# Delta stage written out cycle by cycle, with two places for solved rows, values projected last, and the residual added in the MLP stage

## The reference, cut to what matters

```python
h = rms(x)                                   # x: rows after attention
q, k, v = (silu(silu(causal_conv(h @ W.T))) for each of q, k, v)   # 4 taps
q, k = l2norm per head of 16; beta = sigmoid(h @ Wbeta.T)          # 32 heads
for t in range(32):                          # per sequence and head
    S = S - beta_t * (S k_t - v_t) k_t^T
    o_t = S q_t
x = x + rms(o) @ Wout.T
x = x + (silu(rms(x) @ Wgate.T) * (rms(x) @ Wup.T)) @ Wdown.T
```

## Time and profile before

| | us |
|---|---|
| median of 3 runs (lowest to highest) | 3359.82 (3357.68 to 3363.45) |
| profiled execution, its own time | 3363.44 |
| its span, first to last instruction | 3361.7 |
| attention stage, to | 581.7 |
| delta stage, from 581.7 to | 1860 |
| MLP stage, to | 2657 |
| last stage, to | 3361.7 |

### The profile page before, as it was taken

The page is one execution under the profiler, slowest core; times in us unless marked ns, Lnnn a source line. Parts: engine busy times, 40 slices in busy tenths (PEclk is TensorE's granted clock), DMA queues, the critical chain, the costliest instruction groups (busy, mean ns, idle before and its releaser), DMA issues. The chain is left out here.

```text
span 3361.7 us, 67018 instructions
## 1 busy us (share of the span) xinstructions
PE 2871.6 (85%) x26552; PEld 1584.4 (47%) x26552; DVE 2020.5 (60%) x2996; ACT 1294.6 (39%) x2076; POOL 1111.3 (33%) x742
## 2 busy tenths in 40 slices
PE   6999997686887978788763799999999799999998
PEld 3444443243454544544442344444444366666665
DVE  3444443369979788797884344444443366666665
ACT  2222221455445445444521322222222256666665
POOL 0000000045826447283563000000000077777776
PEclk9999998787988979889775899999999899999999
DMA  6998996100010100101000423222321101111110
GB/s 241 337 332 297 322 329 219 59 20 1 2 39 2 39 17 25 40 2 39 6 24 30 170 89 112 101 82 79 116 88 51 58 29 37 37 40 38 37 41 29
DMA packets 135638, 307.06 MB, mean 91 GB/s; under 512 B 31520, under 2 KB 36384, under 8 KB 131328
## 3 DMA queue, kind: packets, MB, share of 16 engines
q1 hardware_dynamic: 131968, 278.69, 24.1%
q10 hardware_dynamic: 3456, 25.17, 2.2%
HBM read 261.80 MB, written 42.01 MB: 90 GB/s over the span
## 5 line engine op out<-in xcount | busy, mean ns | idle before, releaser
L809 POOL TENSOR_TENSOR b_tmp<-b_L,b_U 128x496 f32<-128x496 f32 (+30 forms) x248 | 259.8, 1048 | 526.5 <-ACT b_L L1035 507.7
L1914 POOL TENSOR_TENSOR d_zb<-d_za 128x1024 f32<-128x1024 f32 x32 | 75.4, 2355 | 1066.3 <-DVE d_za L1970 1066.3
L864 PE MATMUL b_e<-b_hT,b_wqkv 128*128 128x512 f32 x768 | 331.7, 593 | 0.0
L1216 DVE TENSOR_TENSOR b_U<-b_U,b_tmp 128x1488 f32<-128x1488 f32 (+30 forms) x248 | 305.7, 1233 | 8.6
L1214 DVE TENSOR_TENSOR b_tmp<-b_L,b_U 128x1488 f32<-128x1488 f32 (+30 forms) x248 | 286.8, 1156 | 16.9 <-ACT b_L L1035 11.2
L811 POOL TENSOR_TENSOR b_U<-b_U,b_tmp 128x496 f32<-128x496 f32 (+30 forms) x248 | 280.4, 1131 | 19.4
L1449 PE MATMUL c_r<-c_hT,c_g_pair 128*128 128x512 f16 x1056 | 258.4, 397 | 13.3 <-DVE c_hT L1591 13.3
L1600 DVE SCALAR_TENSOR_TENSOR c_av<-c_r,c_sg 128x512 f32<-128x512 f32 x88 | 60.9, 692 | 342.2 <-PE c_r L1449 310.8
L1171 DVE SCALAR_TENSOR_TENSOR b_raw<-b_e,b_cw,b_raw 128x496 f32<-128x496 f32 (+2 forms) x288 | 201.4, 716 | 73.4 <-ACT b_raw L1049 62.7
L1449 PE MATMUL c_r<-c_hT,c_u_pair 128*128 128x512 f16 x1056 | 242.3, 379 | 0.0
L1449 PE MATMUL c_d<-c_d_pair,c_aT 128*128 128x512 f16 x1056 | 241.0, 379 | 0.0
(11 more groups left out here) (223 smaller groups left out, 5391.7 us busy)
## 6 DMA issues: line engine op xcount, KB each, us to landing
a_cT<-in_ctxT SPq DMA_DIRECT2D x128, 512.0 KB, 9.8
a_cn<-in_ctx SPq DMA_DIRECT2D x128, 512.0 KB, 9.3
a_x_ln<-in_x SPq DMA_DIRECT2D x8, 1024.0 KB, 16.5
a_cw<-in_ctx SPq DMA_DIRECT2D x128, 64.0 KB, 9.9
a_x_res<-in_x SPq DMA_DIRECT2D x32, 256.0 KB, 11.2
x<-a_x_out SPq DMA_DIRECT2D x32, 256.0 KB, 11.0
b_xg<-x SPq DMA_DIRECT2D x8, 1024.0 KB, 5.3
b_xr<-x SPq DMA_DIRECT2D x32, 256.0 KB, 2.6
```

Of the source, the lines that this page charges most:

```text
L809: nc.gpsimd.tensor_tensor(tmp[:, QV, s + 1:S, :], lo, us, ALU.mult).then_inc(pool_prod, 1)
L864: mm = pe.matmul(p[:], w_qkv[:, i, k, c * P:(c + 1) * P], hT[:, k, :], start=(k == 0), stop=(k == DC - 1))
L1216: V.tensor_tensor(U[:, 0:QV, s + 1:S, :], U[:, 0:QV, s + 1:S, :], tmp[:, 0:QV, s + 1:S, :], ALU.subtract).then_inc(sub, 1)
L1914: nc.gpsimd.tensor_tensor(o[:, :, 0, :], a[:, :, 0, :], a[:, :, 1, :], ALU.add).then_inc(bf, 1)
```

## The change

- The delta stage's cycles are all written out, with no loop on any engine, and the rings' orders run over the whole stage.
- `U` and the score buffer have two places each. The right sides and the whole system of group k are transposed first in cycle k, before the solved rows of group k-1. `kh` now lies in buffers that are free at that time.
- q and k are projected first, v last; SiLUs of q and k run by block, those of v by pairs of blocks.
- `outer` and `out` are set between other products of TensorE.
- The causal mask is applied in place by ScalarE, as 31 operations of 128 x 128 elements a group, a column of the mask each as scale; GpSimd only solves.
- All `V`, `L` and `U` copies are ScalarE's. ScalarE also scales the output and stores it without the residual, as `om`; VectorE only makes the reciprocals (`scales_out`).
- VectorE's order: q and k taps after solve steps 0, 3, 4, 5; v taps after 5, 6, 7; norms after 7; scaling after 8, 9, 10, 11.
- The MLP stage loads `x1`, `rrow` and `om`; ScalarE rebuilds the residual (`lifted`, after f = 3), VectorE adds `om` (`joined`, f = 4), and `x1` (`doubled`, f = 7). The end of a group has one VectorE operation a tile.

```diff
+    early, late = [], []
+    for g in range(NG):
+        early += [f"{g}.h{c}" for c in range(DC)] + [f"{g}.{i}{c}" for c in range(DC) for i in "qk"]
+        early += [f"{g}.v{c}" for c in range(DC)]
+        for what in ("S0", "S1", "G0", "S2", "G1", "S3", "G2", "G3"):
+            c = what[1]
+            early += ([f"{g}.r{i}{c}" for i in "kqb"] if what[0] == "S" else
+                      [f"{g}.gram{c}.{j}" for j in range(BG)])
+    for k in range(-1, NG + 1):
+        prev, cur, nxt = k >= 1, 0 <= k < NG, k + 1 < NG
+        names = [f"V{i}" for i in range(NV)] + [f"L{i}" for i in range(NL)] if cur else []
+        names += [f"U{i}" for i in range(NV)] if prev else []
+        names += ["beta"] * nxt + ["O0"] * prev + ["ss"] * nxt
+        names += (["O1", "O2", "O3", "power", "total"] + [f"out{t}" for t in range(TG)]) * prev
+        late += [f"{k}.{n}" for n in names]
+    late += ["end"] * (-len(late) % 4)
...
+        kh = [vt_all[:, (DC - 1) * GT:DC * GT]] + [raw[:, c, 2, :] for c in range(DC - 1)]
-        As = sb("As", [P, NU, S])
-        Ah = sb("Ah", [P, NU, S])
+        Am = [sb(f"A{i}", [P, NU, S]) for i in range(2)]
-        U_all = sb("U", [P, NU * HD])
-        U = U_all[:].rearrange("u (q t d) -> u q t d", q=4, d=HD)
-        Uf = U_all[:].rearrange("u (r d) -> u r d", d=HD)
+        U_all = [sb(f"U{i}", [P, NU * HD]) for i in range(2)]
+        Uq = [u[:].rearrange("u (q t d) -> u q t d", q=4, d=HD) for u in U_all]
+        Uf = [u[:].rearrange("u (r d) -> u r d", d=HD) for u in U_all]
...
+                        store(k, t)
+                if k + 2 < NG:
+                    E.take(sp, 0, f"{k + 1}.h{DC - 1}")
+                    if k >= 1:
+                        R.take(sp, 0, f"{k}.out{TG - 1}")
                     load_x(k + 2)
+                    store(k, TG - 1)
...
-            def masks(k):
-                pool.wait_ge(as_copied, DC * BG * (k + 1))
-                for c in range(DC):
-                    R.take(pool, k + 1, f"O{c}")
-                    units = slice(c * UC, (c + 1) * UC)
-                    nc.gpsimd.tensor_tensor(Ah[:, units, :], As[:, units, :],
-                                            past[:].unsqueeze(1).to_broadcast([P, UC, S]), ALU.mult)\
-                        .then_inc(ah_ready, 1)
-            solve(0)
-            masks(0)
-            with pool.Fori(1, NG) as k:
+            for k in range(NG):
                 solve(k)
-                masks(k)
...
+            for k in range(-1, NG + 1):
+                prev, cur, nxt = k >= 1, 0 <= k < NG, k + 1 < NG
+                g = k + 1
+                if cur:
+                    pe.wait_ge(vt_ready, DC * (k + 1))
+                    for i in range(NV):
+                        turned(k, f"V{i}", lambda d: vt[:, :, d])
+                    E.used(pe, 0, f"{k}.gram{DC - 1}.{BG - 1}")
+                    for i in range(LE):
+                        turned(k, f"L{i}", lambda t: Gs[:, t, :])
+                if nxt:
+                    rows(g)
+                if cur:
+                    for i in range(LE, NL):
+                        turned(k, f"L{i}", lambda t: Gs[:, t, :])
+                if nxt:
+                    E.used(pe, 0, f"{g}.h{DC - 1}")
+                    for name in "qk":
+                        project(g, name, 0)
+                if prev:
                     pe.wait_ge(sub, (S - 1) * k)
                     pe.wait_ge(pool_sub, (S - 1) * k)
+                        turned(k, f"U{i}", lambda d: Uf[(k - 1) % 2][:, :, d])
+                if nxt:
+                    betas(k)
+                    for name in "qk":
+                        project(g, name, 1)
+                if prev:
+                    for i in range(NV):
+                        R.used(pe, 0, f"{k}.U{i}")
+                    pe.wait_ge(ah_ready, (S - 1) * k)
+                if nxt:
+                    for name in "qk":
+                        project(g, name, 2)
+                    if prev:
+                        outer(k, 0)
+                    powers(k, 0)
+                    for name in "qk":
+                        project(g, name, 3)
+                    if prev:
+                        outer(k, 1)
+                    project(g, "v", 0)
+                    powers(k, 1)
+                    project(g, "v", 1)
+                    powers(k, 2)
+                    project(g, "v", 2)
+                    project(g, "v", 3)
+                    powers(k, 3)
+                elif prev:
+                    outer(k, 0)
+                    outer(k, 1)
+                if prev:
+                    outer(k, 2)
+                    outer(k, 3)
+                if nxt:
+                    spreads(g, 0)
+                if prev:
+                    power(k)
+                if nxt:
+                    spreads(g, 1)
+                if prev:
+                    total(k)
+                    out(k, 0)
+                if nxt:
+                    if prev:
+                        out(k, 1)
+                    gram(g, 0)
+                    spreads(g, 2)
+                    if prev:
+                        out(k, 2)
+                    gram(g, 1)
+                    spreads(g, 3)
+                    if prev:
+                        out(k, 3)
+                    gram(g, 2)
+                    gram(g, 3)
+                elif prev:
+                    for t in range(1, TG):
+                        out(k, t)
...
+            def masks(k, first, end):
+                act.wait_ge(as_copied, DC * BG * (k + 1))
+                for t in range(first, end):
+                    A.activation(Am[k % 2][:, :, t], Am[k % 2][:, :, t], ACT.Copy, scale=past[:, t:t + 1])\
+                        .then_inc(ah_ready, 1)
+            def store(k, t):
+                p, free = R.take(act, 0, f"{k}.out{t}")
+                if t == 0:
+                    act.wait_ge(os_ready, k)
+                    if k > 1:
+                        act.wait_ge(stored, 16 * TG * (k - 1))
+                A.activation(ov[:, t, :], p[:], ACT.Copy, scale=oscale[:, t:t + 1]).then_inc(free, 1)
...
+            for k in range(-1, NG + 1):
+                prev, cur, nxt = k >= 1, 0 <= k < NG, k + 1 < NG
+                g = k + 1
+                if cur:
+                    for i in range(NV):
+                        right_side(k, i)
+                    if nxt:
+                        rows_normal(g)
+                    for i in range(LE):
+                        system(k, i)
+                if nxt:
                     rows(g)
+                if cur:
+                    masks(k, 0, 8)
+                    for i in range(LE, NL):
+                        system(k, i)
+                if nxt:
+                    tap_first(g, "q", 0)
+                    tap_first(g, "k", 0)
+                if cur:
+                    masks(k, 8, 16)
+                if prev:
+                    for i in range(NV):
+                        spread_u(k, i)
+                if cur:
+                    masks(k, 16, 24)
+                if nxt:
+                    betas(k)
+                    tap_first(g, "q", 1)
+                    tap_first(g, "k", 1)
...
+                    outer(k, 2)
+                if nxt:
+                    silus_v(g, 1)
+                if prev:
+                    outer(k, 3)
+                    power(k)
+                if nxt:
                     masked(g, 0)
-                if do["prev"]:
-                    outer(r, 3)
-                if do["next"]:
+                if prev:
+                    total(k)
+                if nxt:
                     masked(g, 1)
                     copies(g, 0)
+                if prev:
+                    store(k, 0)
+                    store(k, 1)
+                if nxt:
                     masked(g, 2)
                     copies(g, 1)
-                if do["prev"]:
-                    power(r)
-                if do["next"]:
+                if prev:
+                    store(k, 2)
+                if nxt:
                     masked(g, 3)
                     copies(g, 2)
-                if do["prev"]:
-                    total(r)
-                if do["next"]:
+                if prev:
+                    store(k, 3)
+                if nxt:
                     copies(g, 3)
-                if do["prev"]:
...
-            def body(k, do):
-                r = k + 1
-                    right_side(r, 1)
-                    right_side(r, 2)
-                    system(r, LE)
...
                 for s in range(S - 1):
-                    if do["cur"]:
+                    if cur:
                         solve(k, s)
-                    if do["next"] and s in NEXT:
-                        fn, c = NEXT[s]
-                        fn(k + 1, c)
-                    if do["next"] and s == 8:
-                        norms(k + 1)
-                    if do["prev"] and s in (20, 25):
-                        store(k - 1, (0, 1) if s == 20 else (2, 3))
```

(60 more changed lines are left out.)

483 lines of the change are left out of this document (194 added, 289 removed).

## The result

The kernel after takes 3263.6 us, median of 4 runs (3261.4 to 3266.8), against 3358.8 (3357.5 to 3363.5) for the kernel before on the same chip: ratio 0.9715, 95% interval 0.9698 to 0.9732. Forecast were 3257, and 3210 to 3315.

The account below looks back on a forecast made before the run. TensorE was to become the delta cycle's bound, at 130 us. Terms +6 (prologue), -6 (cycle 0), -80.6 (cycles 1 to 6), -12 (cycle 7), -12.5 (MLP) gave -105, from 3363.4 to 3258; predicted 3257, range 3210 to 3315.

Parts of the forecast that it names:

- The cycle of 130 us: Delta cycles 1 to 6: TensorE's 123.5 us, 5 idle, about 1.5 handovers, 130 against 143.4; saves 80.6 us.
- Gaps in `outer`: TensorE's outer products: four blocks of 256 keep a gap of about 2 us each, 8 us a cycle, despite unrolling.
- Rival 1: TensorE's gaps vanish between long products and its clock stays up: cycle 120 to 123 us, total 3209 or 3196; chance 0.12.
- A mask at 0.45 us: ScalarE's mask operation of 128 columns, by a straight line through 512 and 1024 columns: 0.45 us, eight take 3.6.
- VectorE: Delta cycle: 106 us busy, about 112 alone, plus 16 of waits: about 3 for v taps, 13 before blocks 0, 2, 3.
- The signs named in advance: Right: cycles 128 to 132 us, TensorE share over 0.88, MLP transposes waiting 1. Wrong: VectorE over 8 before block 2.
- Prologue: Before the first solve (138.9 us): ScalarE's chain gains 8 us, norms come 2 us earlier; +6.
- Cycle 0 and 7: Delta cycle 0: masks' slowing -5, seam -6, new waits +5, -6. Cycle 7: solve instructions 8.3 and output rows 4, -12.
- MLP stage: Seven group boundaries 2.3 us each, -16; stage's end -2.4; added start load and `doubled(0)` +5.7; sum -12.5.
- 2, ScalarE as the late link: Delta cycle: masks cost 0.73 us or ring banks are held longer; cycle 136 to 140 us, 3293 to 3317; chance 0.22.
- 4, the seam that stays: Between solves: L7 waits behind masks, only loops' and masks' us saved; 3311 us or more, up to no change; chance 0.06.
- 3, the lower clock through the whole block: TensorE at its lower clock from `spreads` 0 to the last gram: 24 us more, cycle 154, 3401 us; chance 0.05.

Follow-up runs that it names:

- The kernel without masks: Kernel after with the causal mask on the delta stage's query products left out (outputs not the reference's): 3229.0 us, ratio 0.9608 to before.
- the kernel after once more: Kernel after, unchanged, measured a second time beside the kernel before as the yardstick: 3262.1 us, ratio 0.9706.
- the part alone: Kernel before with only the MLP part: x1 loaded ahead and doubled, one operation per tile at a group's end: 3343.1 us, ratio 0.9948.
- the kernel with one place: Kernel after with a single `U`, solved rows turned and spread ahead of the next right sides: 3368.2 us, ratio 1.0026 to before.
- three moves: Kernel after with spreads before the second eight masks, outputs one place later, third and fourth outer groups halved between v projections: 3220.9 us, ratio 0.9576 to before.
- two further ones: Added separately to the three moves: next rows before the fifth transpose of L, 3221.3 us; square ahead of silus with root and reciprocal earlier, 3216.7 us.
- the mended order: The three moves plus ScalarE's square of the fourth outer group ahead of silus, root and reciprocal earlier: 3216.7 us, ratio 0.9572 to before.

## Why the prediction was right

The time was right to 6.6 us (3263.6 for 3257), but that close only by luck: the six cycles saved 58.9 us where the sum had 80.6, and the prologue (8.7 us better than forecast), cycle 0 (3.5), the MLP stage (3.5) and attention, which nothing touched (3.0), made up for it. The mechanism (TensorE becomes the bound of the delta cycle) holds for this kernel in three tests: a wait of 2.9 us taken out of TensorE's row shortens the cycle by 4.3 (134.3 to 130.0, the rest is mostly busy time), 14 us taken out of VectorE's waits shorten nothing, and 4.7 us of work added to VectorE cost nothing in the cycle.

- **The cycle of 130 us** was sized 3.6 too low on average, 4.3 in the five cycles with all parts. Term by term there: TensorE's idle time over the seam 2.5 for 5; handovers 0.6 for 1.5; gaps 10.8 for 8; busy time 117.4 for 115.5 (some products at the lower clock, last section); and 2.9 for a wait that the forecast did not have, before `betas`. In all 134.2 for 130. For the missing one I had listed ScalarE's order up to L5 to L7 and stopped there, though eight more masks stood ahead of the spread of `U`. With them moved behind it the cycle is 130.4.
- **Gaps in `outer`**: right that unrolling doesn't remove them (40.8 us in five cycles before, 48.2 after, 24 and 23 gaps). The Trainium skill, "Runtime: NRT & Kernel Launch", section "Instruction fetch mechanics", calls the crossing of a block of 256 instructions mostly hidden; if these gaps are such crossings, that is so for 128 small products between projections (no gap), and not in 256 in a row (one gap, mostly of 2 us or more) or 512 (three of 2.1 to 2.4 us in the third cycle). Rival 1's mechanism exists, then, but needed another order than this change made.
- **A mask at 0.45 us**: measured 3.51 us for 8, 0.44 from start to start. So the bound by rows held, and the 0.29 that the Trainium skill, "VectorE: DVE Perf Modes", section "The TRN2 errata", gives is not what this trace shows.
- **VectorE**: 106 us busy forecast, 107.9 measured. It waits 23.4 us a cycle rather than 16: 7.6 for the taps where 3 was forecast, 14.8 before blocks 0, 2 and 3 for 13. No product of 1008 columns takes 3 us (1.18).
- **The signs named in advance**: three of being right were missed by a little, cycles of 133.6 for 128 to 132, a busy share of 0.874 (five cycles) for over 0.88, a wait of the MLP's transposes of 1.56 us for 1. And one of being wrong was met: VectorE waits 10.0, 8.8 and 8.9 us before block 2 in cycles 1, 2 and 5 (5.3, 7.0 and 5.3 in 3, 4 and 6), over the 8 named. That wait hangs on TensorE's first output products, which stand ahead of `spreads` 2: 16 records of them take 10.12, 8.85 and 8.98 us in those cycles and 7.1 at the full clock. The forecast had counted them at the full clock.
- **The loops**: the sum took cycle 6 of before (139.4) as free of loop costs and the others as 4.3 above it; alone, loops are worth about 20 us in all, 3.2 per cycle.
- **Prologue**: wrong in sign, +6 forecast, -2.7 measured. The added ScalarE work is there (27.0 us from the last block's scaling to the first solve product, 21.1 before), but with q and k first the square root comes 83.8 us after the stage's first load in place of 90.1, 6.3 us where I had allowed 2, and the scaling behind it takes 2.2 less. The kernel without masks has 133.6, but the kernel after once more 132.0, so what the masks cost here is not shown.
- **Cycle 0 and 7**: -6 and -12 forecast, -9.5 and -11.4 measured. In cycle 0 the seam went nearly whole.
- **MLP stage**: -12.5 forecast (its terms, -16, -2.4 and +5.7, add up to -12.7), -16.0 measured, and -17 as the median of the part alone. From the stage's start to its first gate products 29.0 us for 23.9 (+5.1, forecast +5.7); the seven group periods together 650.5 for 669.8 (-19.3, forecast -16); from there to the next stage 100.3 for 102.1 (-1.8, forecast -2.4). The mis-sized term is the boundary, 2.8 us each for 2.3: the wait before the transposes gives 1.9 of it.
- **The rivals**: 2, ScalarE as the late link, is in part what happened, through its order rather than its rate (2.9 us a cycle, not 6 to 10). 4, the seam that stays, is what the kernel with one place shows. 3, the lower clock through the whole block, did not, but single pieces run at the lower level: eight records of a projection behind a gap in 6.60 us where others take 3.70.

## What to carry to other kernels

Add up the busy time and the waits of each engine over one period; the engine for which waits are fewest is the first candidate for the chain. Take one wait out of its row, and one out of a rival's: only what shortens the period was in the chain. When work moves to another engine, go through that engine's order to the end of the period, not to the first meeting point: the 14 us of masks were harmless except for 3.5 us ahead of four copies. A second buffer at a seam can be worth more than everything around it (15 us of 134 a cycle here), and it is what made moving the seam's work to one engine affordable.

After that, removing waits paid less and less: three moves won 44 us, two further ones nothing beyond noise: the waits came back at other places. The kernel with the three moves (3221 us) and the one with the mended order (3217 us) both beat the kernel after by 1.3 to 1.4%.

## What the runs showed of the hardware

Small products (32x32) come at 3.7 to 4.0 us per 128 over a long run. Between two gaps of about 2 us lie 128 of them: TensorE's timeline of the kernel after, third cycle.

```profile
1157.59 1.99 PE L896 MATMUL b_r<-b_A,b_Up 32*32 32x32 f32 x213
1161.89 1.30 PE L896 MATMUL b_r<-b_A,b_Up 32*32 32x32 f32 x128 [2.31 <-issue]
1165.64 1.93 PE L896 MATMUL b_r<-b_A,b_Up 32*32 32x32 f32 x128 [2.44 <-issue]
1169.66 0.85 PE L896 MATMUL b_r<-b_A,b_Up 32*32 32x32 f32 x43 [2.09 <-issue]
```

With the same products in halves between projections of v (three moves together), 128 take 1.29 us and the next large ones follow at once:

```profile
1119.31 1.29 PE L896 MATMUL b_r<-b_A,b_Up 32*32 32x32 f32 x128
1120.53 3.70 PE L845 MATMUL b_e<-b_hT,b_wqkv 128*128 128x512 f32 x8
```

That these gaps are instructions arriving late is the reading that fits; no run here measured the fetching itself.

And the clock may give back or take what a shorter wait wins. In the kernel after, a gap of 2.31 us is followed by eight records of a projection in 6.60 us, and the next eight take 3.70:

```profile
1270.96 0.54 PE L896 MATMUL b_r<-b_A,b_Up 32*32 32x32 f32 x24 [2.31 <-issue]
1271.43 6.60 PE L845 MATMUL b_e<-b_hT,b_wqkv 128*128 128x512 f32 x8
...
1278.94 3.70 PE L845 MATMUL b_e<-b_hT,b_wqkv 128*128 128x512 f32 x8
```

The granted clock is 0.55 from 1271.5 to 1278.0 and 1.00 from 1279.0 to 1282.6: the first eight run at the lower of the clock's two levels, 1.2 and 2.4 GHz, nearly to their end. The gap of 2.31 us at 1161.89 has no such stretch behind it: the clock stays at 1.00 there and falls to 0.50 only in the next gap, 2.44 us, so that 128 small products take 1.30 us before it and 1.93 behind it. From 1111.4, behind the betas, to 1163.9 the third cycle has 1.00 throughout; the fourth, with its gap of 2.31 us in the second group, has 0.90 over the same part (1238.2 to 1291.0) and 0.76 over the next 29 us. Why one gap lowers the clock and another doesn't stays open.
